# Attention and routed experts on one core: where the expert weights are loaded and split, and how the first and last batches are ordered

## The reference

```python
x = x + attention(layernorm(x))   # 16 heads of 8; instead of exp a cubic "stablemax":
                                  # s = 1/(1 - d(1 - d/2 (1 - d/3))), d = logit - row maximum, normalised by its sum
x = x + experts(layernorm(x))     # router picks 2 of 4 experts by top-k of a softmax over 4 logits
# expert e: (silu(y @ w1[e]) * (y @ w3[e])) @ w2[e], w1, w3: [4, 128, 512], w2: [4, 512, 128], fp32
```

## Time and profile before

| | |
|---|---|
| median of 3 executions | 1208.34 us (1206.82 to 1209.16) |
| the profiled execution | 1212.56 us, its span 1210.8 us |
| PE busy | 1134.5 us (94%) |
| ACT busy | 1001.7 us (83%) |
| DVE busy | 997.0 us (82%) |
| POOL busy | 730.1 us (60%) |
| mean granted TensorE clock | 0.993 |

### The profile page before, as it was taken

How to read it: one execution, slowest core, us unless ns; L and a number is a source line. 1 busy time by engine, 2 the same in 40 slices (tenths; PEclk the granted TensorE clock), 3 DMA queues, 4 the chain that set the end, 5 groups by cost and what they waited for, 6 DMA issues and landing times.

```text
span 1210.8 us, 29497 instructions
## 1 busy us (share of the span) xinstructions
PE 1134.5 (94%) x10116; PEld 984.2 (81%) x10116; DVE 997.0 (82%) x1838; ACT 1001.7 (83%) x1001; POOL 730.1 (60%) x959
## 2 busy tenths in 40 slices
PE   2679999999999999999999999999999999999988
PEld 1447888888888888888888888888888888888877
DVE  5778888988888898888889888888988888898732
ACT  1378898888889888888988888998888889888862
POOL 6114666665656666565666656567666565766555
PEclk9988999999999999999999999999999999999999
DMA  5212212222221122222112222211222221122000
GB/s 177 64 62 79 63 51 65 79 84 84 84 63 48 61 78 84 84 83 65 49 59 78 84 84 84 67 55 50 78 84 84 84 68 54 50 78 81 28 23 27
DMA packets 92907, 84.89 MB, mean 70 GB/s; under 512 B 11784, under 2 KB 87240, under 8 KB 92872
## 3 DMA queue, kind: packets, MB, share of 16 engines
q1 hardware_dynamic: 92152, 83.79, 22.0%
q10 hardware_dynamic: 720, 0.66, 0.2%
HBM read 62.20 MB, written 21.10 MB: 69 GB/s over the span
## 4 chain that ended last, share of the span: by engine, by line
PE 62%; POOL 9%; issue 9%; DVE 8%; DMA 5%; ACT 3%; DVEq 2%; SPq 1%; ACTq 0%; POOLq 0%
PE up L867 18%; PE up L1042 10%; PE sc L933 9%; PE pv L883 9%; POOL hid L384 6%; DVE mx L718 4%; PE sc L1026 4%; DMA gate_all<-gate_scratch 3%; PE pv L867 3%; DVEq L709 2%; POOL xn L436 2%; PE misc L1094 1%; PE misc L1075 1%; DVE poly L628 1%; ACT silu_a L506 1%
## 5 line engine op out<-in xcount | busy, mean ns | idle before, releaser
L384 POOL TENSOR_TENSOR hid<-hid,gate_all 128x512 f32<-128x512 f32 x256 | 403.0, 1615 | 201.2 <-DMA gate_all<-gate_scratch 157.4
L498 ACT ACTIVATE w_sq<-sc 128x1024 f32<-128x1024 f32 x256 | 259.4, 1027 | 140.2 <-PE sc L933 138.6
L628 DVE SCALAR_TENSOR_TENSOR poly<-w_sq,sc 128x1024 f32<-128x1024 f32 x256 | 311.7, 1218 | 58.0 <-ACT w_sq L498 49.4
L718 DVE TENSOR_REDUCE mx<-sc 128x4 f32<-128x1024 f32 x256 | 299.7, 1214 | 32.2 <-PE sc L1026 30.7
L1042 PE MATMUL up<-w_sb,hid 128*128 128x128 f32 x2048 | 269.8, 281 | 0.6 <-POOL hid L384 0.6
L867 PE MATMUL up<-xn_hi,w_hi 128*128 128x256 f32 x832 | 253.8, 305 | 2.2 <-ACT silu_a L506 1.5
L555 ACT ACTIVATE poly<-poly,two 128x2048 f32<-128x2048 f32 x128 | 254.9, 1991 | 0.4
L1042 PEld LDWEIGHTS up<-w_sb,hid 128*128 128x128 f32 x2048 | 243.0, 192 | 12.5 <-POOL hid L384 0.8
L560 ACT ACTIVATE poly<-poly 128x2048 f32<-128x2048 f32 x128 | 242.6, 1896 | 0.0
L867 PE MATMUL up<-xn_hi,w_lo 128*128 128x256 f32 x832 | 234.2, 282 | 0.0
L867 PE MATMUL up<-xn_lo,w_hi 128*128 128x256 f32 x832 | 233.5, 281 | 0.0
(11 more groups left out here) (100 smaller groups left out, 1382.0 us busy)
## 6 DMA issues: line engine op xcount, KB each, us to landing
qk_scratch<-qk_split SPq DMA_DIRECT2D x32, 512.0 KB, 3.5
gate_all<-gate_scratch SPq DMA_DIRECT2D x32, 512.0 KB, 5.2
k_pad<-qk_scratch SPq DMA_DIRECT2D x254, 64.0 KB
q_stack<-qk_scratch SPq DMA_DIRECT2D x124, 128.0 KB
x_in<-in_L_attn_x_dram SPq DMA_DIRECT2D x32, 128.0 KB, 2.1
x_res<-in_L_attn_x_dram SPq DMA_DIRECT2D x32, 128.0 KB, 2.3
out_dram<-y_acc SPq DMA_DIRECT2D x32, 128.0 KB, 2.2
poly<-in_L_ffn_w_dram SPq DMA_DIRECT2D x2, 1024.0 KB, 6.9
```

The costliest lines, as they stand in the source:

```text
L384: nc.gpsimd.tensor_tensor(h, h, by_token.unsqueeze(1).to_broadcast([128, 2, C, 128]), ALU.mult).then_inc(gated, 1)
L498: nc.scalar.activation(w_sq[:, u % 2, :], sc[:, u % 2, :], ACT.Square).then_inc(sq_ok, 1)
L628: nc.vector.scalar_tensor_tensor(poly[:, u, :], w_sq[:, u % 2, :], 3.0, sc[:, u % 2, :], ALU.add, ALU.mult).then_inc(poly_ok, 1)
L718: nc.vector.tensor_reduce(by_row[:, :, 2 * g:2 * g + 2], sc[:, u % 2, :].rearrange("p (j k t) -> p j k t", j=2, k=2), AX.X, ALU.min, negat ...
```

## The change

1. `expert_weights` takes the loads of w1, w3 and w2 out of `other_weights`. SP issues them at n = -1, behind batch 0's reads into `k_pad`. w1 and w3 land in `hid`, the experts' activations. The copies to the high parts on ACT move behind the Newton operands of n = -1, and the subtractions for the low parts move from DVE to POOL, behind `blank_stacks(1)`.
2. In `blank_stacks(0)` the first memset waits for `xn_ok` too, no longer only the second.
3. On SP the store of `qk_split` goes ahead of the two DMAs of ones.
4. In step 0, PE transposes the maxima of batch 1 before it does the first two groups of batch 0's weighted values, and the third group goes behind the values of batch 2 in step 1.
5. In step 32, DVE does `xn2` and splits it from PSUM; POOL's eighth gating goes behind the reciprocal deviation; PE transposes after four `down` groups.

```diff
         def blank_stacks(eng, par):
-            eng.memset(q_stack[par][:].bitcast(F32), 0.0).then_inc(blank[par], 1)
             if par == 0:
                 eng.wait_ge(xn_ok, 1)
+            eng.memset(q_stack[par][:].bitcast(F32), 0.0).then_inc(blank[par], 1)
...
-                sp.dma_start(poly[:, 0:2, :].rearrange("p a (b f) -> p (a b) f", b=2),
+            def expert_weights():
+                sp.dma_start(hid[:, 0:NB // 2, :].rearrange("p (e k) t -> p e (k t)", e=E),
                              w1.rearrange("e d f -> d e f")).then_inc(ld_ups, 16)
...
+                if isinstance(i, int) and n == -1:
+                    expert_weights()
...
+                last_router = isinstance(i, int) and no(i, off) == B
-                if has(i, off - 2):
+                if has(i, off - 2) and not last_router:
                     gate_hidden(no(i, off) - 2, UP - 1)
...
+                if isinstance(i, int) and no(i, off) == -1:
+                    for k, lo, hi in ((0, w1_lo, w1_hi), (1, w3_lo, w3_hi)):
+                        pool.wait_ge(w_hi_ok, k + 1)
+                        nc.gpsimd.tensor_tensor(lo[:].rearrange("p e f -> p (e f)"),
+                                                hid[:, NB // 2 * k:NB // 2 * (k + 1), :].rearrange("p n t -> p (n t)"),
+                                                hi[:].rearrange("p e f -> p (e f)").bitcast(F32),
+                                                ALU.subtract).then_inc(split_ok, 1)
+                if last_router:
+                    gate_hidden(no(i, off) - 2, UP - 1)
...
+                    if isinstance(i, int) and n == B:
+                        dve.wait_ge(b_full, UP * m)
+                        nc.vector.tensor_copy(xn2_hi[:], misc[:, 0:S]).then_inc(xn2_hi_ok, 1)
+                        dve.wait_ge(xn2_hi_ok, m + 1)
+                        nc.vector.tensor_tensor(xn2_lo[:], misc[:, 0:S], xn2_hi[:].bitcast(F32),
+                                                ALU.subtract).then_inc(xn2_lo_ok, 1)
...
-                    low_weights(0, w1_lo, w1_hi)
-                    low_weights(1, w3_lo, w3_hi)
+                if isinstance(i, int) and n == B:
+                    dve.wait_ge(rstd_ok, n + 3)
+                    dve.wait_ge(xn2T_full, n - 1)
+                    for c in range(C):
+                        last = nc.vector.tensor_scalar(xn2[:, c, :], y_acc[(off - 1) % 2][:, c, :], mean_var[:, c, 0:1],
+                                                       rstd[:, c:c + 1], ALU.subtract, ALU.mult)
+                    last.then_inc(xn2_ok, 1)
...
+                if isinstance(i, int) and n == 1:
+                    weighted_values(i, off - 1, 2)
                 if has(i, off - 1):
                     weighted_values(i, off - 1, 3)
...
+                if isinstance(i, int) and n == 0:
+                    maxima_T()
                 if has(i, off):
                     weighted_values(i, off, 0)
                     weighted_values(i, off, 1)
```

More of the change, by code:

```diff
@@ L270, in other_weights @@
                 sp.dma_start(rw[:], router_w).then_inc(ld_bias, 16)
-                sp.dma_start(poly[:, 0:2, :].rearrange("p a (b f) -> p (a b) f", b=2),
+            def expert_weights():
+                sp.dma_start(hid[:, 0:NB // 2, :].rearrange("p (e k) t -> p e (k t)", e=E),
                              w1.rearrange("e d f -> d e f")).then_inc(ld_ups, 16)
-                sp.dma_start(poly[:, 2:4, :].rearrange("p a (b f) -> p (a b) f", b=2),
+                sp.dma_start(hid[:, NB // 2:NB, :].rearrange("p (e k) t -> p e (k t)", e=E),
                              w3.rearrange("e d f -> d e f")).then_inc(ld_ups, 16)
@@ L304, in first_half @@
                 if has(i, off + 1):
+                    after(sp, qk_ok, split)
+                    after(sp, stacked[1 - par], scratch_read)
+                    sp.dma_start(scratch.rearrange("a p t -> p a t"),
+                                 qk_split[:].rearrange("p a t -> p (a t)").rearrange(
+                                     "p (a t) -> p a t", t=S).bitcast(F32)).then_inc(qk_stored, 16)
                     if isinstance(i, int) and 0 <= n + 1 < 2:
@@ L309, in first_half @@
                                          ones[:].unsqueeze(1).to_broadcast([2, GP, S])).then_inc(ones_in[par], 16)
[L310 to L314, removed]
                 if has(i, off - 2):
@@ L432, in second_half @@
                     nc.gpsimd.drain()
-                    for t in range(lo, C if isinstance(i, int) and no(i, off) == -2 else hi):
+                    for t in range(C if last_router else lo, C if isinstance(i, int) and no(i, off) == -2 else hi):
                         dst, src = ((xn2[:, t, :], y_acc[(off - 1) % 2][:, t, :]) if t < C
@@ L443, in second_half @@
                     blank_stacks(pool, off)
+                if isinstance(i, int) and no(i, off) == -1:
[7 more added lines that the diff above has]
+                    gate_hidden(no(i, off) - 2, UP - 1)
                 if has(i, off - 1):
                     m = no(i, off) - 1
+                if has(i, off - 1) and not last_router:
                     pool.wait_ge(xn2_out, m + 1)
@@ L453, in second_half @@
                                             ALU.subtract).then_inc(xn2_lo_ok, 1)
+                if has(i, off - 1):
                     pool.wait_ge(compared, m + 1)
@@ L509, in first_half @@
                 if isinstance(i, int) and n == -1:
[L510 to L513, removed]
                     act.wait_ge(qk_stored, 16)
@@ L573, in second_half @@
                     nc.scalar.activation(rstd0[:, s], ln_var[:, s], ACT.Exp, scale=-0.5).then_inc(rstd0_ok, 1)
+                if isinstance(i, int) and n == -1:
+                    act.wait_ge(ld_ups, 16 * 2)
+                    for k, hi in ((0, w1_hi), (1, w3_hi)):
+                        nc.scalar.copy(hi[:].rearrange("p e f -> p (e f)"),
+                                       hid[:, NB // 2 * k:NB // 2 * (k + 1), :].rearrange("p n t -> p (n t)")
+                                       ).then_inc(w_hi_ok, 1)
                 for g in range(G):
@@ L603, in blank_values @@
                 nc.vector.memset(v_pad[par][:, :, :, 16 + HD], 1.0).then_inc(consts_v, 1)
[L605 to L610, removed]
             def first_half(i, off):
@@ L821, in second_half @@
                     return
-                if isinstance(i, int) and n == -1:
-                    low_weights(0, w1_lo, w1_hi)
-                    low_weights(1, w3_lo, w3_hi)
+                if isinstance(i, int) and n == B:
[5 more added lines that the diff above has]
+                    last.then_inc(xn2_ok, 1)
                 for u in range(U):
@@ L1105, in second_half @@
                 down(1, 1)
+                if isinstance(i, int) and n == B:
+                    router_operand()
                 down(2, 0)
@@ L1109, in second_half @@
                 down(2, 1)
-                if has(i, off - 1):
+                if has(i, off - 1) and not (isinstance(i, int) and n == B):
                     router_operand()
@@ L1122, in second_half @@
                     weighted_values(i, off, 1)
-                if has(i, off + 1):
+                if has(i, off + 1) and not (isinstance(i, int) and n == 0):
                     maxima_T()
@@ L1130, in second_half @@
                     up_b_unit(i, off - 1, 0)
-                if has(i, off):
+                if has(i, off) and not (isinstance(i, int) and n == 0):
                     weighted_values(i, off, 2)
```

## The result

The changed kernel takes 1213.29 us (median of 9 executions, 1212.02 to 1215.78), the kernel before in the same runs 1208.66 us (9 executions, 1206.82 to 1211.27). The ratio is 1.0040, with a 95% interval of 1.0028 to 1.0052: 4.8 us slower (3.4 to 6.3). The forecast was 1209.7 with a range from 1205 to 1212.3, and the highest chance on a difference of less than 0.2%. The time lies above the range. The profiled execution took 1215.78 us, the longest of the nine, its span 1214.0, against 1212.56 and 1210.8.

The account below looks back on a forecast made before the run. PE was busy 94% of the span, the start bound by a single thread of waits. New wait +1.3, steps 0 and 1 +0.8, step 32 -0.7: +1.4 us on the median 1208.34 gave 1209.7, range 1205 to 1212.3.

Parts of the forecast that it names:

- x and the store: Start, batch 0: two `xn` operations in about 0.45 us, the store landing at 14.6, 3.7 us sooner.
- The reads: Start, batch 0: reads slowed 1.4 us by the weights (bounds 0 to 3), scores beginning at 24.8, 2.3 us sooner.
- rival (a): Start: exclusion does not bite, or subtractions end before the maxima's split; 2.3 us kept, 1206.1 us; chance 0.2.
- The weights' own way: Start: weights issued at 18.4 let ACT start at 27.6 (26.8 to 29); POOL's subtractions end at 38.8.
- The new wait: Maxima's split of batch 0 ends behind POOL's subtractions, 39.2 against 37.85: 1.3 us loss (-2.3 to +2.7).
- Steps 0 and 1: PE's new order brings batch 2's queries and keys 1.7 us later: 0.8 us loss (0 to 1.3).
- Rival (c): Start of step 1: PE's clock stays low, delaying the values' copy; about 4.5 instead of 0.8, 1213.4 us; chance 0.1.
- Step 32: Without the eighth gating in front, DVE's `xn2` operations end at 1180.0 and PE idles 0.5 us: 0.7 us gain.
- the race: Step 32: DVE's first `xn2` operation starts, POOL's gating follows; DVE's second must not find POOL in it, else 0.8 loss.
- Rival (d): Step 32: DVE's second `xn2` operation waits for POOL's gating; gain becomes 0.8 us loss, 1211.2 us; chance 0.15.

Follow-up runs that it names:

- The three parts apart: Three kernels, each the kernel before with only parts 1 to 3, only part 4 or only part 5 of the change: ratios 1.0031, 1.0011 and 1.0003.
- queries first: The kernel before with only part 4, and the queries and keys of batch 2 put ahead of the weighted values: ratio 1.0014.

## Why the prediction was wrong

The three parts apart lose 3.7, 1.3 and 0.4 us, in sum 5.4, in agreement with the 4.8 (3.4 to 6.3) of the whole. The prediction had +1.3, +0.8 and -0.7.

1. **x and the store: right.** `xn` in 0.52 us (0.45 said), the split's end at 11.82 (11.75), the store issued at 11.85 (11.8) and landed 2.88 us later (2.80), the reads issued from 14.75 (14.6).
2. **The reads: the price was too low.** I took 1.4 us for the weights beside them; they landed 2.7 us later than alone (7.33 against 4.66), within the bound of 3. The scores began at 26.2, not at 24.8. In the forecast itself this cost had dropped out, because POOL decided there. In rival (a) it had not: with the wait gone, the traces have the mark of batch 0 only 0.6 to 0.8 us sooner than the mean of the four with the old start, not 2.3, though the timed 2.1 us (0.7 to 3.4) of that kernel does not exclude the 2.3.
3. **The weights' own way: the step that failed.** It said 27.6 for ACT's start and measured 29.54. I had added 0.6 us to the free time of 8.6 for the reads still in flight; the runs show 11.0 with the reads and 8.26 without. In the prediction's terms it is 9.2 us for a term that measured 11.0: I charged the reads for the weights and did not charge the weights as much for the reads. POOL's subtraction was right (4.6 said, 4.52 measured).
4. **The new wait: the mechanism right, the size wrong by the step above.** The split waited for POOL's running subtraction and ended with it. Its end was put at 39.2 and came at 40.78: +2.9 instead of +1.3 us, beyond even the bound of +2.7. Moving the subtractions away removes the wait, and cutting them into pieces shortens it to the rest of a piece, as the exclusion asks. The argument was made from the second operation, which reads two operands in SBUF. The wait of 3.98 us fell on the first, which reads only `mx`; the second found POOL idle and took 0.19 us. In the run with pieces both waited.
5. **Steps 0 and 1: right in direction, at the upper bound in size.** 0.8 said (0 to 1.3), 1.3 timed (0.2 to 2.5). The queries did come 1.7 us later, between the medians of the traces. The 0.5 us that I took off for an earlier rise of the clock was counted from a trace in which it rose late: its third group of `pv`, at 72.44, took 1.93 us for 16 matmuls, and 1.07 in the other six traces of that order. The prediction let the reads alone decide; queries first shows that something else, perhaps the values' copy, stands close behind. Rival (c), in which the clock stays low through step 1, did not occur: the third and fourth groups took 1.93 us for 32 matmuls in all five traces with part 4. That its price, 1213.4, lies next to the measured 1213.29 is chance.
6. **Step 32: the wrong side of the race.** The forecast had DVE's two operations done before POOL's gating. The first was, the second, starting 0.13 us after the gating, waited for its end. So it was in all four kernels that have this order, each with 1.80 us. With POOL held off, the step gains 0.84 us against the one trace of before, and 0.4 to 0.5 against the median of seven (0.7 said). Rival (d) had the loss at 0.8; the traces have 0.7 against the median, and timed is 0.4 with an interval of -0.7 to 1.5. The clock's fall to 0.50 in the changed kernel's profile, which the prediction did not have for this place, occurred in one of the four traces with the lost race: in the other three the gap was 1.60 or 1.61 us, not 1.86, and 24 matmuls took 2.84. It can't be said how many of the timed executions it touched.
7. **The range.** It ended at 1212.3, 1.1 us beyond rival (d), and measured is 1213.29. Of the 3.4 us by which the shift was missed (+1.4 said, +4.8 measured), 1.6 are the new wait, 0.5 steps 0 and 1, and 1.1 step 32, in sum 3.2. The stated upper bounds of the three terms, with the race lost, add up to 2.7 + 1.3 + 0.8 = 4.8 us, 1213.1. I had not let them fall together, though nothing kept them apart, and rival (c), with a chance of 0.1, was left outside the range.

## What to carry to other kernels

Work moved onto GpSimd isn't free because GpSimd is idle. A long operation there can hold up a short one of VectorE that reads SBUF: here subtractions of 9.0 us on GpSimd, taken off VectorE, put 3.8 us on a critical operation of 0.18 us. So put it where VectorE works from PSUM only, or cut it into pieces. Where nothing waits for bulk loads, issue them after the critical reads have landed: behind them in the queue is not behind them in time. When two transfers are laid beside each other, charge both. And a difference of a microsecond between two single traces needs more traces, unless executions of one kernel are known to agree up to there.

## What the runs showed of the hardware

- DVE waits for the one POOL operation that runs, not for POOL to become idle: 1.07 and 1.20 us beside pieces of 1.26 us, 3.98 in one of about 4.5. The Trainium skill (SBUF — State Buffer, Who interferes with whom) has the exclusion for the whole instruction, and the traces agree. It has it for a DVE instruction with two SBUF inputs and for one in a 2-port mode, which it says `tensor_scalar` can enter; the operation of 3.98 us is a TENSOR_SCALAR with one input, and no row here shows its mode.
- Starting first protects one operation only. Two DVE operations issued back to back around the start of a POOL operation took 0.345 and 1.541 us in the changed kernel, and 1.80 us together in all four kernels with that order.
- Reads and weights in flight together slow each other. The last read, issued by ACT, lands 7.33 us after its issue beside the weights that SP issued, 4.58 without them; 2 MB of weights need 11.0 us beside the reads, 8.26 without.
